# Rows of u and B for the scan's matmuls: 36 rows three partitions apart in two loads, or 40 rows in six loads

## The chip, the cores and the metric

One core of one Trainium2 chip runs the kernel. The metric is the device time of one execution in microseconds, lower is better; the kernel before takes 1117.4 us in the median of three runs (1115.65 to 1119.68).

## The reference

A Mamba block beside a small binary MLP, on x of shape 8 x 512 x 128, with E = 256 inner channels and N = 64 states. What matters here is the scan over T = 512 steps:

```python
normed = rmsnorm(layernorm(x)); x_z, z = split(normed @ in_proj_W)
xc = silu(conv(x_z)); dt = clip(softplus(xc @ dt_W + dt_b), 0.001, 0.1)
Bp, Cp = xc @ B_W, xc @ C_W
def step(h, ins):                        # h: 8 x 256 x 64, float32
    dA = exp(dt_t[..., None] * A)
    h = dA * h + dt_t[..., None] * B_t[:, None, :] * x_t[..., None]
    y_t = einsum('ben,bn->be', h, C_t)
```

Then y * silu(z), an output projection, a gated FFN, and the sum with the MLP and x.

## The kernel before

**Two stages.** A first stage handles the eight batches one after the other (`batches`): norms, projections, convolution, dt, and u = dt * xc. u and B are split into three bf16 parts each (`u_parts`, `b_parts`), whose nine products give the float32 product u * B on the matmul. The parts are stored to DRAM (`u_stage`, `b_stage`), dt as well (`dt_stage`). The second stage is the scan: 16 bodies of STEPS = 32 steps; three are written out, twelve stand in a loop of four turns with three bodies each, one is written out at the end.

**One step.** ScalarE (ACT) makes exp(dt * A) in place in `decay`, two steps at a time (L1011), two steps ahead, and copies half of the state out of PSUM (L1031). GpSimd (POOL) multiplies one half of the state with the decay (L593), VectorE (DVE) adds the product u * B that TensorE (PE) left in PSUM (L1238), and multiplies the other half in PSUM (L1227), onto which PE accumulates its product (L743 accumulates, L750 is the other half's). PE contracts the state with C (L798). Between these lie the output stages of the steps before (`finish_groups`).

**The rows of a product.** A product matmul contracts over 64 partitions, 0 to 63 for one half (`rows(0)`) and 64 to 127 for the other. 18 of the 64 hold a pair (part i of u, part j of B) for one of two batches; the rest is zero, set once. `moving` holds u, `b_rows` holds B with two layouts `hq` of the halves. The 36 rows of one `hq` stand three partitions apart from 10 + hq on (`product_rows`), both halves in one load. A chunk has TC = 16 steps and two buffers `cb`; for each chunk and `hq` there is one `load_u` (L194) and one `load_b` (L201), so 4 loads for 16 steps. In `moving` both `hq` have rows of their own.

**The queue.** All DMAs are issued by SyncE (SP), in program order. Besides the chunks it loads the decay: for each two steps one pair of loads of 512 KB (L392), into one of NDEC = 6 slots, as soon as `self_state` says that the slot's old steps are done. In one body (32 steps) SP issues 32 decay loads, 8 chunk loads, 2 `x_in` and 2 `out`. In `body` the loads of `hq` 0 stand ahead of the decay loads for steps 2 and 4, those of `hq` 1 behind these and ahead of the one for step 6; the same again 16 steps later. PE waits in `wait_chunk` for all loads of a chunk, ACT for its two decay loads.

**Between the stages.** SP stores for the last batch u (L417), issues the first four decay loads, stores B and the last part of u, waits until all have landed (L431), and issues the loads of chunk 0, eight decay loads, the loads of chunk 1.

## Time and profile before

| | us |
|---|---|
| median of three runs | 1117.4 |
| the profiled execution, its own time | 1104.51 |
| its span, first to last instruction | 1102.7 |
| PE, DVE, ACT, POOL busy | 965.8, 915.7, 922.8, 849.0 |
| mean granted TensorE clock | 0.952 |
| DMA moved | 327.40 MB, mean 297 GB/s |

The busy times are shares of one span: four engines are each busy for 77% to 88% of it, so none is alone the bound, and the stage that is looked at decides. The profiled execution is 12.9 us (1.2%) shorter than the median of the runs; sums below are made against it and then moved to the median.

### The profile page before, as it was taken

To read this page: it belongs to the slowest core of one execution; us is meant where nothing else is said; L and a number is where in the kernel's file an instruction comes from. 1 tells how busy PE (TensorE), PEld (TensorE's weight loads), DVE (VectorE), ACT (ScalarE), POOL (GpSimd) and SP (SyncE) were. 2 spreads that over 40 slices of the span, in tenths; PEclk is the share of its full clock that TensorE was granted. 3 is DMA by queue.
4 is the path that set the end of the run, shared out by engine and by line. 5 is a ranking of instruction groups with operands and counts; after the bars stand their busy time and mean duration, and the time that the engine had idled before them with its cause. 6 is when DMAs were issued, how large, how long until landed. Compare 5 with 4: busy or idle time off the path is not lost.

```text
span 1102.7 us, 27634 instructions
## 1 busy us (share of the span) xinstructions
PE 965.8 (88%) x8006; PEld 425.0 (39%) x8006; DVE 915.7 (83%) x2035; ACT 922.8 (84%) x1125; POOL 849.0 (77%) x1216
## 2 busy tenths in 40 slices
PE   5988983668999999997999997999999899999898
PEld 3565540113343433332334343334333334343436
DVE  5677663798989999997999997898998799899992
ACT  1656775689999999997999997999998899999981
POOL 6555523688888888897898887888888798889880
PEclk9999996679999999999999999899999899999999
DMA  5234358999999999998899999899999799999940
GB/s 140 81 139 165 142 202 300 327 319 353 341 345 344 338 355 350 344 352 316 315 355 354 345 348 344 290 346 358 339 350 344 272 354 352 345 343 350 350 158 11
DMA packets 76759, 327.40 MB, mean 297 GB/s; under 512 B 13472, under 2 KB 32800, under 8 KB 41504
## 3 DMA queue, kind: packets, MB, share of 16 engines
q1 hardware_dynamic: 76576, 325.30, 83.1%
q8 instruction: 73, 1.20, 0.4%
q14 instruction: 110, 0.90, 0.2%
HBM read 303.24 MB, written 22.02 MB: 295 GB/s over the span
## 4 chain that ended last, share of the span: by engine, by line
PE 32%; DVE 26%; POOL 19%; issue 14%; ACT 3%; DMA 3%; SPq 2%; DVEq 1%; POOLq 0%; ACTq 0%
POOL decayed L593 13%; PE ps L798 11%; DVE ps L1227 8%; PE ps L743 7%; DVE state L1238 6%; PE ps L883 5%; PE ps L897 5%; DVE h L1335 2%; DVE soft L1153 2%; DMA decay<-dt_stage 1%; POOL soft L543 1%; PE ps L861 1%; PE ps L869 1%; ACT state L1031 1%; DVE gated L1300 1%
## 5 line engine op out<-in xcount | busy, mean ns | idle before, releaser
L593 POOL TENSOR_TENSOR decayed<-decay,state 128x256 f32<-128x256 f32 x1024 | 726.6, 735 | 158.4 <-DVE state L1238 113.9
L1011 ACT ACTIVATE decay<-decay,a_col 128x2048 f32<-128x2048 f32 x256 | 513.9, 2008 | 31.8 <-DMA decay<-dt_stage 18.5
L1238 DVE TENSOR_TENSOR state<-decayed,ps 128x256 f32<-128x256 f32 x1024 | 405.7, 416 | 62.7 <-POOL decayed L593 41.1
L1227 DVE TENSOR_TENSOR ps<-decay,ps 128x512 f32<-128x512 f32 x512 | 352.3, 688 | 38.9 <-ACT state L1031 12.2
L798 PE MATMUL ps<-state,c_cols 128*32 128x256 f32 x4096 | 341.8, 407 | 0.0
L1031 ACT COPY state<-ps 128x512 f32<-128x512 f32 x512 | 288.3, 588 | 57.0 <-issue 37.6
L743 PE MATMUL ps<-moving,b_rows 64*128 64x256 bf16 x1024 | 206.4, 283 | 91.9 <-DVE ps L1227 88.9
L750 PE MATMUL ps<-moving,b_rows 64*128 64x256 bf16 x1024 | 207.4, 284 | 12.2 <-DMA b_rows<-b_stage 12.2
L883 PE MATMUL ps<-h,w 128*128 128x256 f32 x512 | 175.9, 429 | 0.8 <-DVE h L1335 0.8
L743 PEld LDWEIGHTS ps<-moving,b_rows 64*128 64x128 bf16 x1024 | 58.2, 95 | 268.9 <-DVE ps L1227 164.1
L798 PEld LDWEIGHTS ps<-state,c_cols 128*32 128x32 f32 x4096 | 82.4, 110 | 115.0 <-issue 104.5
L883 PEld LDWEIGHTS ps<-h,w 128*128 128x128 f32 x512 | 79.7, 191 | 92.8 <-issue 89.7
L750 PEld LDWEIGHTS ps<-moving,b_rows 64*128 64x128 bf16 x1024 | 57.5, 95 | 12.6 <-DMA moving<-u_stage 12.5
L652 PE MATMUL ps<-n_feat,w_tap 128*128 128x512 f32 x128 | 58.9, 614 | 1.0 <-ACT n_feat L917 1.0
L897 PE MATMUL ps<-w,h 128*128 128x128 f32 x256 | 44.6, 299 | 0.3 <-ACT h L1071 0.3
L848 PE MATMUL ps<-xn_feat,w 128*128 128x256 f32 x128 | 44.2, 429 | 0.3 <-DVE result L1344 0.2
L679 PE MATMUL ps<-w_dt,xc_feat 128*128 128x256 f32 x128 | 35.9, 439 | 8.5 <-ACT xc_feat L927 8.5
L897 PEld LDWEIGHTS ps<-w,h 128*128 128x128 f32 x256 | 33.5, 191 | 24.8 <-issue 24.0
L679 PEld LDWEIGHTS ps<-w_dt,xc_feat 128*128 128x128 f32 x128 | 32.1, 328 | 12.3 <-ACT xc_feat L927 10.3
L652 PEld LDWEIGHTS ps<-n_feat,w_tap 128*128 128x128 f32 x128 | 24.6, 198 | 29.8 <-issue 29.8
L1153 DVE TENSOR_TENSOR soft<-soft 128x1024 f32<-128x1024 f32 x8 | 20.8, 2602 | 16.3 <-POOL soft L543 16.3
L1113 DVE TENSOR_SCALAR normed<-x_tok,mean_var,nrm 128x128 f32<-128x128 f32 x32 | 19.9, 753 | 15.6 <-POOL nrm L534 15.6
(124 smaller groups left out, 813.3 us busy)
## 6 DMA issues: line engine op xcount, KB each, us to landing
decay<-dt_stage SPq DMA_DIRECT2D x512, 512.0 KB, 6.5
moving<-u_stage SPq DMA_DIRECT2D x64, 288.0 KB
b_stage<-b_parts SPq DMA_DIRECT2D x24, 384.0 KB, 3.7
b_rows<-b_stage SPq DMA_DIRECT2D x64, 144.0 KB
dt_stage<-dt_tok SPq DMA_DIRECT2D x8, 512.0 KB, 3.2
u_stage<-u_parts SPq DMA_DIRECT2D x8, 512.0 KB, 2.8
x_tok<-in_L_attn_x_dram SPq DMA_DIRECT2D x4, 512.0 KB, 3.6
u_stage<-u_parts SPq DMA_DIRECT2D x8, 256.0 KB, 2.1
```

The lines of the kernel that those rows point to most:

```text
L593: nc.gpsimd.tensor_tensor(decayed[:, p], decay[:, dec_slot(m, k), p, k % TS, :], state[:, (k - 1) % RING, p * E:(p + 1) * E], ALU.mult).th ...
L652: m = nc.tensor.matmul(ps[:, XC + h, :], w_tap[:, k, h * P:(h + 1) * P], n_feat[:, bass.ds(n, 1), k:k + T].rearrange("d o t -> d (o t)"), ...
L679: m = nc.tensor.matmul(ps[:, DTT + j // 2, (j % 2) * E:(j % 2 + 1) * E], xc_feat[:, bb, h, j:T:NJ], w_dt[:, h, :], start=(h == 0), stop=(h ...
L743: return nc.tensor.matmul(ps[:, acc_bank(m, k), p * E:(p + 1) * E], b_rows[rows(1), cb, p, kk, :], moving[rows(1), cb, kk, :], start=False ...
L750: return nc.tensor.matmul(ps[:, SELFP + k % 2, p * E:(p + 1) * E], b_rows[rows(0), cb, p, kk, :], moving[rows(0), cb, kk, :], start=True, ...
L798: m = nc.tensor.matmul(ps[q * 32:(q + 1) * 32, YP, 0:E], c_cols[:, cb, q, kk * 2 * TC:(kk + 1) * 2 * TC], state[:, k % RING, q * E:(q + 1) ...
L883: m = nc.tensor.matmul(ps[:, FB, c * GTOK:(c + 1) * GTOK], w1[:, n, f:f + P], h1[:, n, :], start=(n == 0), stop=(n == H1 // P - 1))
L897: m = nc.tensor.matmul(ps[:, FB, j * P:(j + 1) * P], terms[c][0][:, j * P:(j + 1) * P], terms[c][1], start=(c == 0), stop=(c == len(terms) ...
L1011: nc.scalar.activation(pair, pair, ACT.Exp, scale=a_col[:, 2:3]).then_inc(decay_ready, 1)
L1031: nc.scalar.copy(state[:, k % RING, SELF:QE], ps[:, acc_bank(m, k), :]).then_inc(acc_copied, 1)
L1227: nc.vector.tensor_tensor(ps[:, acc_bank(m, k), :].rearrange("p (q e) -> p q e", q=HQ), decay[:, dec_slot(m, k), HQ:Q, k % TS, :], ps[:, a ...
L1238: nc.vector.tensor_tensor(state[:, k % RING, p * E:(p + 1) * E], decayed[:, p], ps[:, SELFP + k % 2, p * E:(p + 1) * E], ALU.add).then_inc ...
```

## The change

For one `hq`, 32 rows stand on every second partition from 32 to 95, in 16 blocks of four partitions (two `hq`, two products). A block has one u row, loaded to both of its partitions, and two B rows. In DRAM the parts of u stand in the order 0, 2, 1, 2 (NS = 4 rows in place of 3); B has a plane for each of its parts, with the rows in the order of the blocks. This holds seven of nine products and one row of zeros (the blank, stored once from the zeroed `moving`). The two others (u parts 0 and 1 with B part 2) stand outside, on partitions 0 to 15 and 96 to 111, in four more loads of four rows each. So 40 rows in 6 loads for one `hq`, where there were 36 rows in 2. No matmul changes its shape.

```diff
-            sp.dma_start(moving[product_rows(hq), cb].rearrange("r t e -> r (t e)"),
-                         u_stage[hq, :, :, :, bass.ds(t, TC), :].rearrange("f b i t e -> (f b i) (t e)")
-                         .unsqueeze(1).broadcast_to([HALF * NP, NP, TC * E])
+            sp.dma_start(moving[window_rows(hq), cb].rearrange("r t e -> r (t e)"),
+                         u_stage[hq, :, :, :, bass.ds(t, TC), :].rearrange("f b s t e -> (f b s) (t e)")
+                         .unsqueeze(1).broadcast_to([BLOCKS, 2, TC * E])
                          ).then_inc(chunk_loaded[cb], 16)
...
-            sp.dma_start(b_rows[product_rows(hq), cb, hq].rearrange("r t n -> r (t n)"),
-                         b_stage[hq, :, :, :, :, bass.ds(t, TC), :].rearrange("f b i j t n -> (f b i j) (t n)")
+            sp.dma_start(b_rows[window_rows(hq), cb, hq].rearrange("r t n -> r (t n)"),
+                         b_stage[0:2, hq, :, :, :, bass.ds(t, TC), :].rearrange("r f b s t n -> (f b s) r (t n)")
                          ).then_inc(b_loaded[cb], 16)
+
+        def load_outer(sp, t, cb, hq):
+
+            for f in range(2):
+                sp.dma_start(moving[outer_rows(hq, f), cb].rearrange("r t e -> r (t e)"),
+                             u_stage[hq, f, :, 0:NP:2, bass.ds(t, TC), :].rearrange("b s t e -> (b s) (t e)")
+                             ).then_inc(chunk_loaded[cb], 16)
+                sp.dma_start(b_rows[outer_rows(hq, f), cb, hq].rearrange("r t n -> r (t n)"),
+                             b_stage[2, hq, f, :, 0:NP:2, bass.ds(t, TC), :].rearrange("b s t n -> (b s) (t n)")
+                             ).then_inc(b_loaded[cb], 16)
+
+        def load_chunk(sp, t, cb, hq):
+
+            load_u(sp, t, cb, hq)
+            load_b(sp, t, cb, hq)
+            load_outer(sp, t, cb, hq)
...
-                            [(u_parts, u_stage[q % HQ, q // HQ, bb], 0, 2, "u_mid_ready")]
-                            + [(b_parts, b_stage[q % HQ, q // HQ, bb, i], 0, NP, "b_split") for i in range(NP)]
-                            + [(u_parts, u_stage[q % HQ, q // HQ, bb], 2, 3, "u_split")]):
+                            (u_rows[0:NP:2], u_parts[:, bb, 0:2], 1, "u_mid_ready"),
+                            (b_planes[0, 0:NP], b_parts[:, bb, 0:1], NP, "b_split"),
+                            (b_planes[1, 0:NP], b_parts[:, bb, 1:2], NP, "b_split"),
+                            (b_planes[2, 0:NP:2], b_parts[:, bb, 2:3], 2, "b_split"),
+                            (b_planes[0, NP:NS], b_parts[:, bb, 2:3], 1, "b_split"),
+                            (u_rows[1:NS:2], u_parts[:, bb, 2:3], 2, "u_split"))):
...
+                            sp.wait_ge(blank_zeroed, 1)
+                            sp.dma_start(b_stage[1, :, :, :, NP].rearrange("a f b (p j) n -> p (a f b) (j n)", j=NJ),
+                                         moving[:, 1].rearrange("p t e -> p (t e)").rearrange("p (k n) -> p k n", k=B)
+                                         ).then_inc(blank_stored, 16)
```

On SP's queue, the last batch's stores and the loads of chunk 0, before (each row is an engine's instruction with its line, what it writes and reads, partitions x elements, and how many in a row):

```order
L417 DMA b_stage<-b_parts 128x3x512 x3
L417 DMA u_stage<-u_parts 128x1024
L194 DMA moving<-u_stage 36x1x4096
L201 DMA b_rows<-b_stage 36x2048
L194 DMA moving<-u_stage 36x1x4096
L201 DMA b_rows<-b_stage 36x2048
L392 DMA decay<-dt_stage 64x2048 x8
```

The same place on SP's queue after the change:

```order
L447 DMA b_stage<-b_parts 128x3x512 x2
L447 DMA b_stage<-b_parts 128x2x512
L447 DMA b_stage<-b_parts 128x512
L447 DMA u_stage<-u_parts 128x2x1024
L201 DMA moving<-u_stage 32x1x4096
L208 DMA b_rows<-b_stage 32x1x2048
L215 DMA moving<-u_stage 4x4096
L218 DMA b_rows<-b_stage 4x2048
L215 DMA moving<-u_stage 4x4096
L218 DMA b_rows<-b_stage 4x2048
```

Six such rows follow for the other `hq`, and then the eight decay loads: eight more issues stand ahead of these, and the last u store writes twice as much.

In a body of the scan, on SP's queue from the loads of `hq` 0 to the decay loads behind those of `hq` 1, before:

```order
L194 DMA moving<-u_stage 36x1x4096
L201 DMA b_rows<-b_stage 36x2048
L392 DMA decay<-dt_stage 64x2048 x4
L194 DMA moving<-u_stage 36x1x4096
L201 DMA b_rows<-b_stage 36x2048
L392 DMA decay<-dt_stage 64x2048 x12
```

And after, from the same place on:

```order
L201 DMA moving<-u_stage 32x1x4096
L208 DMA b_rows<-b_stage 32x1x2048
L215 DMA moving<-u_stage 4x4096
L218 DMA b_rows<-b_stage 4x2048
L215 DMA moving<-u_stage 4x4096
L218 DMA b_rows<-b_stage 4x2048
L415 DMA decay<-dt_stage 64x2048 x4
```

The next six chunk loads follow in the same way. Each group of decay loads now has four more issues ahead of it; the rows of the other engines differ in nothing but their line numbers.

## Rows read from the trace of the kernel before

**Rows 1.** The page: busy us (share of the span) by engine; the data queue.

```profile
PE 965.8 (88%) x8006; PEld 425.0 (39%) x8006; DVE 915.7 (83%) x2035; ACT 922.8 (84%) x1125; POOL 849.0 (77%) x1216
...
q1 hardware_dynamic: 76576, 325.30, 83.1%
```

**Rows 2.** Windows: stretch, its length, busy time by engine, clock, DMA share, GB/s.

```profile
160.00:173.50 13.50, 7.64 (x22) 3.07 (x20) 1.58 (x2) 10.97 (x14) 0.00 (x0) 0.93 0.88 301
173.50:184.00 10.50, 1.62 (x10) 0.61 (x10) 3.27 (x8) 0.53 (x1) 3.30 (x5) 0.50 0.73 231
184.00:195.00 11.00, 6.15 (x56) 1.62 (x56) 8.06 (x18) 9.33 (x11) 7.96 (x12) 0.64 1.02 342
195.00:206.00 11.00, 4.88 (x48) 1.15 (x44) 5.73 (x13) 6.19 (x7) 5.62 (x8) 0.67 1.00 367
...
357.00:520.00 163.00, 147.72 (x1394) 61.22 (x1390) 145.78 (x339) 151.12 (x185) 140.17 (x208) 1.00 0.98 349
```

**Rows 3.** ACT's waits by line, 166 to 206 us.

```profile
ACT decay L1011 <- DMA decay<-dt_stage: 16.5, 4, 10.7
```

**Rows 4.** ACT's waits by line, 206 to 1068 us, the scan's rest.

```profile
ACT decay L1011 <- DMA decay<-dt_stage: 2.0, 2, 1.4
```

**Rows 5.** SP's queue in time: start, us, what, how many; between the stages.

```profile
165.01 0.84 SPq L417 DMA_DIRECT2D u_stage<-u_parts  x1
173.53 0.95 SPq L194 DMA_DIRECT2D moving<-u_stage  x1
...
176.99 5.89 SPq L392 DMA_DIRECT2D decay<-dt_stage  x8
```

**Rows 6.** PE and ACT in time, the first that wait for these loads.

```profile
180.99 0.37 PE L750 MATMUL ps<-moving,b_rows 64*128 64x256 bf16 x1 [12.23 <-DMA b_rows<-b_stage]
...
184.70 2.00 ACT L1011 ACTIVATE decay<-decay,a_col 128x2048 f32<-128x2048 f32 x1 [10.67 <-DMA decay<-dt_stage]
```

**Rows 7.** SP's issues by line: duration ns min/median/max.

```profile
L392 SPq DMA_DIRECT2D decay<-dt_stage x512: 471/476/1482, 160.7 to 1055.8; - x171
...
L194 SPq DMA_DIRECT2D moving<-u_stage x64: 778/839/948, 173.5 to 1029.1; - x64
...
L201 SPq DMA_DIRECT2D b_rows<-b_stage x64: 730/778/797, 174.5 to 1029.9; - x64
...
L446 SPq DMA_DIRECT2D x_in<-in_L_attn_x_dram x32: 631/652/1099, 207.9 to 1044.0; - x32
```

**Rows 8.** DMA issues: count, KB each, median us to landing where known.

```profile
decay<-dt_stage SPq DMA_DIRECT2D x512, 512.0 KB, 6.5
moving<-u_stage SPq DMA_DIRECT2D x64, 288.0 KB
...
b_rows<-b_stage SPq DMA_DIRECT2D x64, 144.0 KB
```

**Rows 9.** SP's waits, 206 to 1068 us: total, times, longest.

```profile
SPq L392 <- DVE state L1238: 162.4, 98, 2.3
SPq L135 <- DVE state L1238: 134.0, 72, 5.6
```

**Rows 10.** SP's queue in time, one body of the scan.

```profile
701.15 1.63 SPq L452 DMA_DIRECT2D out_dram<-result  x2
...
717.98 0.84 SPq L194 DMA_DIRECT2D moving<-u_stage  x1
...
720.68 4.32 SPq L392 DMA_DIRECT2D decay<-dt_stage  x4
725.18 0.84 SPq L194 DMA_DIRECT2D moving<-u_stage  x1
726.22 0.77 SPq L201 DMA_DIRECT2D b_rows<-b_stage  x1
...
755.75 1.63 SPq L452 DMA_DIRECT2D out_dram<-result  x2
```

**Rows 11.** ACT in time, the exp of the pair issued at 666.6 us.

```profile
678.17 2.00 ACT L1011 ACTIVATE decay<-decay,a_col 128x2048 f32<-128x2048 f32 x1 [0.65 <-DMA decay<-dt_stage]
```

More of the change, by code:

```diff
@@ L46, in mamba_and_binary_mlp_block @@
     HROW = P // 2
[L47 to L50 removed]
+    NS = NP + 1
+    BLOCKS = 2 * HQ * NS
+    WFIRST, BSTEP = P // 4, P // 2 // BLOCKS
+    assert BLOCKS == 16 and BSTEP == 2 * HQ
     QE = Q * E
@@ L416, in store @@
                         wait_all(sp, [(S[ready], n + 1)])
-                        sp.dma_start(stage[i0:i1].rearrange("i (p j) e -> p i (j e)", j=NJ),
-                                     parts[:, bb, i0:i1].rearrange("p i j e -> p i (j e)")
+                        rows = parts.rearrange("p i j e -> p i (j e)")
+                        if copies > 1:
+                            rows = rows.broadcast_to([P, copies, rows.shape[-1]])
+                        sp.dma_start(stage.rearrange("i (p j) e -> p i (j e)", j=NJ), rows
                                      ).then_inc(S[f"parts_stored{bb}"], 16)
```

50 lines of the change are left out of this document (24 added, 26 removed).

## The prediction

> **What bounds the kernel now.** I read the page first. No engine is busy for more than 88% of the span, and the data queue fills 83.1% of what 16 DMA engines could do in it [rows 1]. A share over the whole span says little, so the windows come next: three stretches differ. Between the stages (160 to 184 us) all engines but ACT stand nearly idle while DMA moves 231 to 301 GB/s; from 184 to 206 us the scan has started and the DMA share is 1.0 at 342 and 367 GB/s; in the scan proper it is 0.98 at 349 GB/s, and PE, DVE, ACT are each busy over 89% [rows 2]. So the scan is tuned to engines and DMA at once. Who waits decides: ACT waits 16.5 us for decay loads before 206 us [rows 3] and only 2.0 us in the 862 us behind [rows 4]. Between the stages the path is: the last u store is issued at 165.01 us, SP sees it landed at 173.53, issues the four loads of chunk 0 until 176.99 [rows 5], PE starts at 180.99, and ACT, which has done two pairs, gets the third pair of decay at 184.70 [rows 6]. There DMA and SP set the time; in the scan they are hidden, but with little in hand.
>
> **The change part by part.**
>
> *Stores.* Each batch stores four planes of u in place of three, 256 KB more, in six issues in place of five; B's planes remain nine. For seven batches this lies beside engines' work, since SP only waits there for the next result. Behind the last batch it is on the path: 262 kB at the 301 GB/s of that stretch [rows 2] is +0.9 us. Bounds: 0.5 us (at 367 GB/s with some of it under the issue), 1.7 us (when the seventh batch's extra bytes are still queued too). The blank, 1 MB, is stored when SP has nothing else to do; were its DMA in the way, it would be 3 us of a stage in which DMA moves far less than it can. I cost it at nothing.
>
> *Chunk 0.* Twelve issues replace four. Four took 3.46 us (173.53 to 176.99), 0.81 us each and 0.05 between [rows 5]. How long SP needs for 32 or 4 rows, no row shows. The bounds are the shortest and the longest median: 0.476 us for the 64 rows of a decay load, 0.839 for 36 rows of u; `x_in` has 0.652 [rows 7]. For the 32-row loads, cut in 16 blocks, I take the decay's 0.48; for the four-row loads, an odd shape like `x_in`, 0.65. That gives 4 x 0.53 + 8 x 0.70 = 7.7 us, +4.3 us (ends: 12 x 0.53 = 6.3, +2.9; 12 x 0.89 = 10.7, +7.2). PE starts 4.0 us after SP is through with the old four [rows 5, 6]. A part of these 4.0 us is queueing: 864 KB within 3.5 us is more than the DMA engines move in it. Spread over 7.7 us that falls, by somewhat under 1 us. The eight decay loads are issued later by the same amount, and ACT waits for the first of them at once. I take +3.5 us of the 4.3 (ends 1.5 and 7).
>
> *Chunk 1.* 96 KB more in a full queue, at 342 GB/s [rows 2] +0.3 us. Its issues take 4.3 us longer too, but stand behind eight decay loads: 4.2 MB, 12 us of DMA at 342 GB/s, issued in 5.9 us [rows 5]. These 6 us in hand hide the 4.3. If the cover were gone, ACT's next waits would grow by what is left.
>
> *The scan, SP's time.* A body takes 54.6 us (701.15 to 755.75) and SP spends 1.03 us from one u load's issue to the next, of which 0.84 is the issue and 0.19 registers [rows 10, 7]. Eight 36-row issues become eight 32-row ones, 8 x (0.48 - 0.81) = -2.6 us, and 16 four-row ones come in, 16 x (0.65 + 0.19) = +13.4: +10.8 us a body. SP waits 296 us for DVE's state in 862 us [rows 9], 18.8 us a body (15.8 bodies). 8 us remain; at the upper price of 0.84 us it is 16.5 us with nothing saved, still under 18.8. So SP isn't the bound on average.
>
> *The scan, the late loads.* What is queued behind the six issues are the decay loads. With 4.7 us for six issues (2 x 0.67 + 4 x 0.84) where two took 2.1, the timeline of [rows 10] reads: `hq` 0 ends at 722.7 and not before 720.68, 2.0 us late; four decay loads back to back (4 x 0.66) bring SP to 725.4, 0.2 us late; `hq` 1 ends at 730.1 in place of 727.3, 2.8 us late. The pair behind it is the tightest of the body: the one issued at the same place at 666.6 us was waited for by ACT at 678.17 [rows 11]. But a load lands 6.5 us after its issue in the median [rows 8], and this one took 11.5: some 5 us of it is other loads ahead in full DMA engines. A load that is issued 2.8 us later then meets 2.8 us less of queue and lands at the same time. What stays is bytes: 432 KB for one `hq` [rows 8] become 480, 192 KB a body, 0.56 us at 349 GB/s. Over 15.8 bodies that is 8.9 us if DMA sets the pace, and 0 if the slack that left only 2.0 us of waits [rows 4] holds. As the tightest pairs have no slack already, I take two thirds, +6 us (ends: 0; 35, in the first rival).
>
> *PE.* Same matmuls on the same 64 partitions. PE waits for a chunk's last load in step 15 of 16; `hq` 1 is now issued by step 8 of them, with over 10 us to land. Nothing.
>
> The sum against the profile's own time: 0.9 + 3.5 + 0.3 + 6 = +10.7, 1104.5 to 1115.2 us. The median of the runs is 12.9 us above that execution; I add the same 10.7 to it: 1128.1 us.
>
> **A rule weighed against this.** In the rows, SP needs 0.84 and 0.78 us to issue 36 rows and 0.48 for 64 [rows 7]: the old loads are of an odd kind. The Trainium skill, "DMA: Bandwidth & Descriptors", section "Why a DMA increments its semaphore by 16 and not by 1", says that a load runs on the largest number of engines, up to 16, that divides the outer size on both sides. By that rule the old loads ran on 12 engines, the 32-row loads run on all 16, and four-row loads on the lowest four alone. No row of this profile tells engines apart. It speaks for the window and against the outer loads; by it the first rival holds, and the sum would be 1143 us rather than 1128.
>
> **The rivals.**
>
> *Four engines carry the outer loads (slower, more).* A load of four rows has four pieces to hand out; if each piece goes to one engine and always to the same ones, those hold back every decay load, which is landed only when its slowest engine is done. For: nothing in the change spreads them. Against: if the pieces are cut finer, it is nothing. Price: in a body such an engine moves 1024 KB of decay, 96 of the window, 384/4 = 96 of outer loads, 16 of `x_in` and `out`: 1232 KB, 1.262 MB. An engine moves 22.2 GB/s while busy (325.30 MB in 83.1% of 16 x 1102.7 us [rows 1]), or 22.9 at the peak of 367 [rows 2]: 56.8 or 55.1 us against 54.6. That is +0.5 to +2.2 us a body, +8 to +35; with its middle, 21, and the 4.7 us ahead of the scan, 1143 us. It decides once an engine's own load passes 54.6 us of work.
>
> *The better layout pays (faster).* Each block of four partitions is written by an engine of its own, and 16 rather than fewer engines share the window. If this lets all transfers run faster, the 16.5 and 2.0 us of ACT's waits [rows 3, 4] and part of PE's are there to win, and in the unprofiled runs perhaps some of the 12.9 us that the profile doesn't have. Against: the chunk loads are 1.7 MB of the 7.8 MB that move from 184 to 206 us; at half their cost that wins 2.4 us, less than the 4.7 that the issues and the stores cost. It decides only if decay loads gain too, by 8.1 of 18.5 us of waits for a gain beyond the bound. Price: 12 us won, 4.7 lost, 1110 us.
>
> The Trainium skill, "SBUF — State Buffer", section "Door 1: The DMA port swizzle", says that four neighbouring partitions share one DMA port and that 32 to 95 reach all 16 ports. By that rule the window is written without two engines on a port, but the decay loads' rows, nine times the bytes in a body, are where they were. It adds nothing to the sum.
>
> *Covered (no change).* Four-row issues at the lower price, queueing that shrinks as issues spread, slack that takes the bytes: 0.9 + 1.5 us, 1120 us.
>
> **How the numbers follow.** Forecast 43% (1122 to 1137), four engines 22% (1137 to 1158), faster 15% (1103 to 1114), covered 20%. 0.3% is 3.4 us, about what a measurement of this kernel tells from no change. Slower 0.65, same 0.20, faster 0.15. The range of 8 in 10 leaves out most of the faster case and the top of the four-engine one: 1113 to 1150.
>
> **What would show it.** In the changed profile: the last u store lands about 9.3 us after its issue, before 8.5; SP's issues of chunk 0 take some 7.7 us, with 0.48 and 0.65 us by line; PE's first product comes at about 185.5 us; ACT's waits for decay grow from 2.0 to some 8 us in the scan; SP's waits for the state fall by half. If these waits grow to tens of microseconds and a load's landing from 6.5 to over 8, four engines are overloaded. If the waits before 206 us fall under 16.5, the layout pays. Wrong would make me: four-row issues of over 1 us, which put SP itself over its 18.8 us, or a decay load that now lands sooner.

## The result, and the profile after

The changed kernel takes 1101.83 us (median of four runs, 1098.49 to 1103.92), the kernel before beside it 1116.53 us (1112.67 to 1119.68): ratio 0.9894, 95% interval 0.9845 to 0.9943. A second measurement later gave 1101.98 us and 0.9902 (0.9869 to 0.9934). It is faster by 1%; the forecast was 1128 us, slower, in a range from 1113 up. Both the direction and the range were wrong. A time below is the median of all executions of a kernel, but a ratio goes by those within 1.5% of its fastest; only for off_48 do the two differ by more than 1 us (1141.96 us over its six executions, 1133.62 over the three that count).

The page of the changed kernel, busy time and data queue, to set beside [rows 1]:

```profile
PE 954.4 (87%) x8006; PEld 422.2 (38%) x8006; DVE 914.5 (83%) x2035; ACT 922.1 (84%) x1125; POOL 847.5 (77%) x1216
...
q1 hardware_dynamic: 80816, 331.60, 81.2%
```

More bytes, 331.60 MB in place of 325.30, took a smaller share of a shorter span (1099.7 us). Not all of these bytes are in the scan: by the sizes of the loads a body of it has 18560 KB where it had 18368, 1.0% more; the rest is stores of the first stage. Bytes over (share x 16 x span) give what one DMA engine moves while it is busy: 23.2 GB/s where it was 22.2. I call this the engine's rate below; it is worked out in this way for each run.

The windows of the kernel after, the stretches of [rows 2]:

```profile
173.50:184.00 10.50, 0.00 (x0) 0.00 (x0) 1.07 (x2) 1.13 (x1) 1.40 (x2) 0.50 0.38 123
184.00:195.00 11.00, 5.41 (x38) 1.46 (x38) 7.02 (x16) 6.29 (x8) 6.68 (x10) 0.50 0.97 371
195.00:206.00 11.00, 6.34 (x72) 1.86 (x72) 8.27 (x19) 8.69 (x11) 8.83 (x13) 0.93 0.98 378
...
357.00:520.00 163.00, 147.38 (x1386) 61.00 (x1379) 145.32 (x338) 149.75 (x184) 139.72 (x206) 0.99 0.93 350
```

The first stretch became emptier (123 GB/s for 231): SP spends it on issues. The next two move 371 and 378 GB/s for 342 and 367. In the scan 350 GB/s need a share of 0.93 where 349 needed 0.98.

SP's queue between the stages after the change, against [rows 5]:

```profile
166.72 0.60 SPq L447 DMA_DIRECT2D u_stage<-u_parts  x1
175.06 0.60 SPq L201 DMA_DIRECT2D moving<-u_stage  x1
175.72 0.59 SPq L208 DMA_DIRECT2D b_rows<-b_stage  x1
176.35 0.71 SPq L215 DMA_DIRECT2D moving<-u_stage  x1
...
182.87 5.02 SPq L415 DMA_DIRECT2D decay<-dt_stage  x8
```

PE and ACT in time, against [rows 6]:

```profile
184.42 0.37 PE L779 MATMUL ps<-moving,b_rows 64*128 64x256 bf16 x1 [15.05 <-DMA b_rows<-b_stage]
188.28 2.00 ACT L1040 ACTIVATE decay<-decay,a_col 128x2048 f32<-128x2048 f32 x1 [13.64 <-DMA decay<-dt_stage]
...
203.13 2.00 ACT L1040 ACTIVATE decay<-decay,a_col 128x2048 f32<-128x2048 f32 x1 [2.31 <-DMA decay<-dt_stage]
```

And the exp of the kernel before that answers to the last of these:

```profile
202.77 2.00 ACT L1011 ACTIVATE decay<-decay,a_col 128x2048 f32<-128x2048 f32 x1 [3.77 <-DMA decay<-dt_stage]
```

Chunk 0 is issued from 175.06 to 182.87 us, 7.8 us where it was 3.5; PE starts 3.4 us later and ACT's third pair 3.6 us later; but 15 us on, at its seventh pair, ACT is at the same place in both profiles, 203.13 against 202.77. It looks as if what was lost between the stages came back at once. The control below doesn't bear this out: its seventh pair comes 4.4 us before that of the kernel after.

Then ACT's waits for decay from 206 to 1068 us in the kernel after [rows 4], and SP's waits in the same stretch [rows 9] (total, times, longest):

```profile
ACT decay L1040 <- DMA decay<-dt_stage: 4.6, 9, 0.9
```

```profile
SPq L137 <- DVE state L1267: 96.1, 58, 3.8
SPq L415 <- DVE state L1267: 33.7, 22, 2.3
```

ACT's 4.6 us are more than the 2.0 of [rows 4], so against that profile these waits show no gain; the control below says why. SP waits 130 us in place of 296: it has less time left, as forecast, but some. SP's issues by line, ns min/median/max, to set beside [rows 7]:

```profile
L415 SPq DMA_DIRECT2D decay<-dt_stage x512: 471/512/1837, 161.8 to 1052.9; - x171
...
L201 SPq DMA_DIRECT2D moving<-u_stage x64: 587/600/1052, 175.1 to 1026.2; - x64
...
L218 SPq DMA_DIRECT2D b_rows<-b_stage x128: 577/632/672, 177.1 to 1029.4; - x128
```

### The profile page after: what moved, and what is told of

It is laid out like the page before. It is cut to its first block, busy times and chain, and to the rows that moved or that the text cites. A ratio compares the mean times of both kernels' runs of the same rounds, so it can differ in the third digit from the quotient of the medians.

```text
span 1099.7 us, 28252 instructions
## 1 busy us (share of the span) xinstructions
PE 954.4 (87%) x8006; PEld 422.2 (38%) x8006; DVE 914.5 (83%) x2035; ACT 922.1 (84%) x1125; POOL 847.5 (77%) x1216
## 3 DMA queue, kind: packets, MB, share of 16 engines
q1 hardware_dynamic: 80816, 331.60, 81.2%
## 4 chain that ended last, share of the span: by engine, by line
PE 22%; DVE 21%; POOL 17%; issue 13%; ACT 2%; DVEq 1%; POOLq 0%; ACTq 0%
POOL decayed L622 15%; DVE ps L1256 8%; PE ps L827 7%; DVE state L1267 7%; PE ps L772 5%; PE ps L926 4%; PE ps L912 3%; DVE h L1364 2%; ACT state L1060 1%; PE ps L890 1%; PE ps L898 1%; DVE gated L1329 1%; POOL base L651 1%; POOL f_nrm L646 1%; POOL f_nrm L634 1%
## 5 line engine op out<-in xcount | busy, mean ns | idle before, releaser
L1256 DVE TENSOR_TENSOR ps<-decay,ps 128x512 f32<-128x512 f32 x512 | 352.5, 688 | 34.5 <-ACT state L1060 15.8
L827 PE MATMUL ps<-state,c_cols 128*32 128x256 f32 x4096 | 337.2, 402 | 0.0
L772 PE MATMUL ps<-moving,b_rows 64*128 64x256 bf16 x1024 | 204.2, 280 | 94.3 <-DVE ps L1256 91.3
L779 PE MATMUL ps<-moving,b_rows 64*128 64x256 bf16 x1024 | 205.2, 282 | 15.1 <-DMA b_rows<-b_stage 15.1
L912 PE MATMUL ps<-h,w 128*128 128x256 f32 x512 | 173.0, 423 | 0.8 <-DVE h L1364 0.8
L681 PE MATMUL ps<-n_feat,w_tap 128*128 128x512 f32 x128 | 57.8, 605 | 1.0 <-ACT n_feat L946 1.0
L708 PEld LDWEIGHTS ps<-w_dt,xc_feat 128*128 128x128 f32 x128 | 31.3, 328 | 15.1 <-ACT xc_feat L956 13.8
L1182 DVE TENSOR_TENSOR soft<-soft 128x1024 f32<-128x1024 f32 x8 | 20.8, 2601 | 16.3 <-POOL soft L572 16.3
L572 POOL TENSOR_TENSOR soft<-soft 128x1024 f32<-128x1024 f32 x7 | 17.2, 2453 | 20.6 <-DVE soft L1171 20.6
```

Of the source, the lines that this page charges most:

```text
L681: m = nc.tensor.matmul(ps[:, XC + h, :], w_tap[:, k, h * P:(h + 1) * P], n_feat[:, bass.ds(n, 1), k:k + T].rearrange("d o t -> d (o t)"), ...
L708: m = nc.tensor.matmul(ps[:, DTT + j // 2, (j % 2) * E:(j % 2 + 1) * E], xc_feat[:, bb, h, j:T:NJ], w_dt[:, h, :], start=(h == 0), stop=(h ...
L772: return nc.tensor.matmul(ps[:, acc_bank(m, k), p * E:(p + 1) * E], b_rows[rows(1), cb, p, kk, :], moving[rows(1), cb, kk, :], start=False ...
L779: return nc.tensor.matmul(ps[:, SELFP + k % 2, p * E:(p + 1) * E], b_rows[rows(0), cb, p, kk, :], moving[rows(0), cb, kk, :], start=True, ...
L827: m = nc.tensor.matmul(ps[q * 32:(q + 1) * 32, YP, 0:E], c_cols[:, cb, q, kk * 2 * TC:(kk + 1) * 2 * TC], state[:, k % RING, q * E:(q + 1) ...
L912: m = nc.tensor.matmul(ps[:, FB, c * GTOK:(c + 1) * GTOK], w1[:, n, f:f + P], h1[:, n, :], start=(n == 0), stop=(n == H1 // P - 1))
```

## The experiments

Each run stands beside runs of the kernel before on the same chip, and has a ratio to these. "On the blocks" means the window rows as in the kernel after (32 to 95), "off" means elsewhere. Where an edit leaves products out or changes them, the recorded expectation says so. The runs fell into four questions, in this order.

### 1. Was the profile of before a fair one, and does the place of the rows pay?

**before_again**, the kernel before once more.

> The kernel before, unchanged, as a control. Every theory expects a ratio of 1.00 within 0.5%, and this time a profile of an execution beside its others: if the profiled execution lies near 1104 us while the others lie near 1116, the 12.9 us that the first profile didn't have come from the execution and not from the kernel; if all lie near 1116, its trace shows in ACT's waits for decay loads in the scan (2.0 us before) what the first one did not.

It took 1110.48 us, ratio 0.9994 (0.9948 to 1.004). ACT's waits for decay in it, 206 to 1068 us:

```profile
ACT decay L1011 <- DMA decay<-dt_stage: 30.7, 27, 2.3
```

27 waits and 30.7 us, where the profile that the prediction read had two and 2.0 us [rows 4]. So the first profile was of an execution that happened to miss them. Its span is 1111.7 us, 9.0 more than the first. A decay load lands 7.7 us after its issue in the median, where the first profile had 6.5 [rows 8] and the kernel after has 6.4. The engine's rate is 21.7 GB/s here. The window that [rows 2] ends with reads:

```profile
357.00:520.00 163.00, 146.01 (x1340) 59.16 (x1339) 141.19 (x327) 144.94 (x178) 135.47 (x201) 0.97 0.99 338
```

A share of 0.99 moves 338 GB/s, where the first profile had 349 at 0.98 and the kernel after has 350 at 0.93.

The start of the scan is the other way round. ACT's seventh pair in the control:

```profile
198.77 2.00 ACT L1011 ACTIVATE decay<-decay,a_col 128x2048 f32<-128x2048 f32 x1 [3.40 <-DMA decay<-dt_stage]
```

That is 4.4 us before the kernel after, and so it stays: the tenth pair comes at 208.39 us in the control, at 212.39 in the first profile, at 212.66 in the kernel after. From there to the end of the span they need 903.3, 890.3 and 887.0 us. Against the control the change thus loses 4.3 us at the start and wins 16.3 us in the scan.

**off_port**, the window rows on every third partition:

```diff
-            first = WFIRST + hq
-            return slice(first, first + HQ * (2 * BLOCKS - 1) + 1, HQ)
+            first = 16 + hq
+            return slice(first, first + 3 * (2 * BLOCKS - 1) + 1, 3)
...
-            first = f * (P - WFIRST) + hq
+            first = f * 112 + hq
```

> The changed kernel with its 32 rows of one hq three partitions apart from 16 + hq on, so a block no longer stands on four partitions of its own; the same bytes, loads, order and issues, 16 blocks as before. Theory A (port): the gain comes from where the rows stand in SBUF; then this is back at the kernel before or slower, ratio 0.998 to 1.01, and a busy DMA engine moves about 22.2 GB/s again in place of 23.2. Theory B (spread): the gain comes from 16 even shares of a load, whatever partitions they go to; then the ratio remains about 0.989 and the rate 23.2.

1140.84 us, ratio 1.0225 (1.017 to 1.0279): 39 us more than the kernel after with the same bytes and the same issues. Its data queue, and ACT's waits in the scan:

```profile
q1 hardware_dynamic: 80816, 331.60, 83.1%
```

```profile
ACT decay L1040 <- DMA decay<-dt_stage: 52.0, 39, 3.6
```

The rate is 21.8 GB/s, for 23.2 on the blocks. The costs that the prediction feared are real here; on the blocks they don't show to this extent.

**no_outer**, the four-row loads left out on the blocks (`load_outer` isn't called, `LOADS = HQ`).

> The changed kernel without its four-row loads: the products of u parts 0 and 1 with B part 2 are left out, the rows stay zero. 32 issues of 50 KB and less are gone from two bodies' 48 chunk loads. If the four-row loads cost what I forecast (SP's time, four engines, first start), this is 3 us faster than the changed kernel at the first product and some 5 us at the end, ratio about 0.984; if they are hidden in the scan and the start is recovered, the ratio stays within 0.3% of the changed kernel's, 0.986 to 0.992.

1091.72 us, 0.98 (0.975 to 0.9849): the outer loads cost 10 us on the blocks.

**one_decay**, one decay load of 128 partitions in place of two of 64:

```diff
-                    for bb in range(2):
-                        sp.dma_start(decay[bb:P:2, slot].rearrange("n q t e -> n (q t e)"),
+                    sp.dma_start(decay[:, slot].rearrange("n q t e -> n (q t e)"),
```

> The changed kernel with one decay load of 128 rows (1 MB) for two steps in place of two of 64 rows (512 KB each). SP issues 16 fewer in a body. Theory A (port): an engine's share is eight neighbouring partitions in place of four of every second one, the same two ports' worth, so DMA's rate hardly changes and the gain is SP's time alone: ACT's waits for decay in the scan fall from 4.6 us towards 2, ratio 0.985 to 0.990. Theory C (SP's late issues are what is left of the cost): ratio under 0.985. If a larger load lands later (twice the bytes before ACT may start), it is slower: ratio over 0.992.

1101.3 us, 0.9884 (0.9838 to 0.9931). ACT's waits in the scan fell to 0.2 us and the time stayed: neither SP's decay issues nor what is left of ACT's waits sets the scan's pace after the change. (The recorded theory A takes a share to be eight neighbouring partitions; no row shows which partitions a share has.)

### 2. What do the outer loads cost, and where?

**off_no_outer**, off the blocks and without outer loads (both edits above).

> The kernel after with the window rows moved off their blocks (every third partition from 16 on, as in the run with the rows off port) and without the four-row loads, so two of the nine products are missing; four loads for a chunk, as in the kernel before. It gives the fourth corner of rows on or off their blocks, with or without outer loads. So far: on with 1101.8, on without 1091.7, off with 1140.8 us. If the place of the rows and the outer loads are two separate costs: 1140.8 - 10.1 = 1130 us (1125 to 1136). If the gain of the blocks is there only to hide what the outer loads cost (SP late, queues behind), the place costs little without them: under 1105 us. If the outer loads cost more where the queues are fuller: 1112 to 1122, about the kernel before.

1096.73 us, 0.9854 (0.9806 to 0.9902). This broke the picture that I had: the place is worth 39 us with the outer loads but 5 us without them, and the outer loads cost 44 us off the blocks but 10 on them. The two are no separate costs. Its queue, beside the kernel before:

```profile
q1 hardware_dynamic: 78768, 325.31, 84.5%
```

It moves the bytes of the kernel before in all (325.31 MB for 325.30), with no row on a block of its own, and is 1.5% faster. In a body it moves 1.0% less, 18176 KB for 18368, since some of its bytes are stores of the first stage; by the prediction's price for bytes that is at most 8.9 us of some 16. How the bytes are dealt out could be the rest: by the prediction's count the fullest engine has 1184 KB a body before, 1136 here, 1232 in the kernel after and with the rows off.

That count rests on the number of shares into which a load is cut, and the traces show that: they keep the increments by which DMA raises a load's semaphore while its parts land. On the semaphores of the chunk loads, a load of 36 rows has 13, one of 32 rows 16, one of four rows five, and one of 32 rows from eight source rows (eight_off below) nine. Wherever there are fewer than 16, one of them comes about 1.2 us after the issue, ahead of all data (in eight_off the loads issued at 183.11 and 183.88 us have theirs at 184.26 and 185.00, and no data of them has landed before 194.8). That leaves 12, 16, four and eight shares.

**outer_small**, one step of 16 in each outer load (`[outer_rows(hq, f), cb, 0:1]`, `bass.ds(t, 1)`).

> The kernel after, with the same eight four-row loads a chunk but one of 16 steps in each, so a sixteenth of their bytes and of their pieces' length (two of nine products are right in one step of 16 only). All issues stay. Leaving the loads out won 10.1 us. If SP's time for eight more issues is the cost: 1101 us, within 2. If their bytes, or the four shares in which they are carried, are the cost: 1092 to 1095 us, with ACT's waits for decay in the scan gone.

1100.76 us, 0.9884 (0.9836 to 0.9931).

**outer_wide**, each outer load 16 rows of a quarter of the length:

```diff
-                sp.dma_start(moving[outer_rows(hq, f), cb].rearrange("r t e -> r (t e)"),
-                             u_stage[hq, f, :, 0:NP:2, bass.ds(t, TC), :].rearrange("b s t e -> (b s) (t e)")
+                rows, part = slice(f * (P - WFIRST), f * (P - WFIRST) + BLOCKS), slice(hq * 4, hq * 4 + 4)
+                sp.dma_start(moving[rows, cb, part].rearrange("r t e -> r (t e)"),
+                             u_stage[hq, :, :, :, bass.ds(t, 4), :].rearrange("a b s t e -> (a b s) (t e)")
```

> The kernel after, with the same eight outer loads a chunk and the same bytes, each as 16 rows of a quarter of the length in place of four rows (their rows hold other parts than the products need, so the output differs). Issues and bytes stay, only the number of shares changes. If four shares that fall on few DMA engines are what the outer loads cost: 1092 to 1097 us, ACT's waits in the scan gone. If it is SP's issues or the bytes: 1100 to 1103 us.

1098.74 us, 0.9867 (0.982 to 0.9914). On the blocks the bytes and shares of the outer loads weigh 1 to 3 us, no more than the intervals. By elimination most of the 10 us stays with the mere issues; that isn't shown, and the profiled execution of outer_small took 1096.02 us, 4.7 less than its median.

**early**, four decay loads ahead of SP's wait for the stores:

```diff
+                for c in range(EARLY, EARLY + 2):
+                    load_dt(c, c, [])
                 sp.wait_ge(rows_zeroed, 2)
...
-                for c in range(EARLY, NDEC):
+                for c in range(EARLY + 2, NDEC):
```

> The kernel after, with four of the eight decay loads of the start issued ahead of SP's wait for the stores rather than behind chunk 0; nothing left out. In the profile of after ACT waits 13.6 us for the first of these eight, while DMA moves only 123 GB/s from 173.5 to 184 us. If order at the start is what ACT waits for: its wait near 188 us goes from 13.6 to about 8, PE's first product does not come later than 184.4 by more than 1 us, and 3 to 5 us are won, 1097 to 1099 us. If DMA as a whole sets the pace of the first pairs (1.0 share from 184 us on), the wait moves to the next pairs and the time stays at 1100 to 1103 us.

1098.82 us, 0.9864 (0.9817 to 0.9911), 3 us under the kernel after, as expected, though within the intervals. ACT's waits from 166 to 215 us fell from 16.4 to 4.2 us, and the window between the stages is filled:

```profile
173.50:184.00 10.50, 0.00 (x0) 0.00 (x0) 1.08 (x2) 2.71 (x2) 1.40 (x2) 0.50 0.77 301
```

It moves 301 GB/s for 123. ACT's tenth pair comes at 208.3 us, where it came at 212.7, and the span is 5.1 us shorter: what is won at the start is still there at the end.

### 3. Is it the fullest engine?

**eight_off**, the same 32 rows, each window load from eight source rows repeated four times:

```diff
-                         u_stage[hq, :, :, :, bass.ds(t, TC), :].rearrange("f b s t e -> (f b s) (t e)")
-                         .unsqueeze(1).broadcast_to([BLOCKS, 2, TC * E])
+                         u_stage[:, :, :, 0, bass.ds(t, TC), :].rearrange("q f b t e -> (q f b) (t e)")
+                         .unsqueeze(1).broadcast_to([8, 4, TC * E])
```

> The kernel with the window rows off their blocks and no four-row loads (1096.7 us), with one change: the source of each window load has eight outer rows, each repeated four times, in place of 16 repeated twice. Same rows written, same bytes, same four issues a chunk (the values differ and two products are missing). By the theory of the fullest engine such a load is cut in eight shares in place of 16, and a DMA engine's own bytes in a body set the time once rows stand off their blocks: 1136 KB for 1096.7, 1184 KB for 1114.5 (the kernel before, if its 36 rows are 12 shares), 1232 KB for 1140.8 (with the four-row loads in four shares). With eight shares it is 1024 + 192 + 16 = 1232 KB: 1135 to 1150 us, and tens of us of ACT's waits for decay in the scan. By the theory that all bytes count alike, or that the four-row loads were dear as issues: 1095 to 1099 us.

1145.29 us, 1.0304 (1.0257 to 1.0351), inside 1135 to 1150. Same bytes in a body, same four issues, no outer loads, and 49 us more than off_no_outer. The waits:

```profile
ACT decay L1040 <- DMA decay<-dt_stage: 60.5, 45, 3.2
```

off_no_outer had none in that stretch. SP's own time for such a load, off_no_outer first and then eight_off:

```profile
L201 SPq DMA_DIRECT2D moving<-u_stage x64: 591/620/1222, 174.5 to 1019.8; - x64
```

```profile
L201 SPq DMA_DIRECT2D moving<-u_stage x64: 664/737/1127, 174.8 to 1069.7; - x64
```

117 ns more for each of 128 loads are 15 us at most, not 49, and SP waits 344 us for DVE in this scan.

**eight_on**, the same edit on the blocks.

> The same change, eight outer rows repeated four times, in the kernel after without the four-row loads (1091.7 us), where the window rows stand on their blocks. The fullest engine has 1232 KB here too, but an engine's share now covers whole blocks of its own. If blocks of one engine each make every transfer faster, the extra bytes still fit: 1091 to 1100 us. If a block that is written by another engine than in the kernel after loses the whole gain: 1115 to 1140 us.

1144.29 us, 1.0304 (1.0248 to 1.036): a little beyond the second theory's 1115 to 1140. Rows on the blocks win nothing when eight shares write them, two blocks each by the order of the rows.

**off_48**, 48 rows on every second partition from 16 on, in 16 shares (`broadcast_to([BLOCKS, 3, ...])`).

> The kernel with the window rows off their blocks and no four-row loads (1096.7 us), with 48 rows on every second partition in place of 32 on every third: 16 blocks repeated three times, 16 shares, the same issues (the extra rows add products that don't belong; two products are missing). The fullest engine has 1024 + 144 + 16 = 1184 KB in a body, as in the kernel before, but all 16 have it, so all bytes are 3% more than before. If the fullest engine sets the time: 1110 to 1119 us. If the sum of the bytes sets it: over 1125 us. If shares of 12 were costly in themselves, not by their bytes: 1096 to 1105 us.

1133.62 us, 1.0201 (1.013 to 1.0271). Only the theory of the sum had a place for that (over 1125). The sum is 3.1% more in a body than before (18944 KB), all shares equal. Yet the trace shows unequal ones: of the 32 shares of a pair of decay loads the last lands 5.6 us after the first in the median, for 3.6 in off_no_outer. So some engines lag here although by the count none has more than another. Shares of three rows that lie across blocks may be the reason; that isn't shown, and the profiled execution was one of the longer (1148.90 us).

**off_wide**, off the blocks, outer loads in 16 shares.

> The kernel with the window rows off their blocks and four-row loads (1140.8 us), the outer loads as 16 rows of a quarter of the length (other values than the products need). Same bytes, same issues; the fullest engine has 1024 + 96 + 24 + 16 = 1160 KB in a body in place of 1232. If the fullest engine sets the time once rows are off their blocks: 1100 to 1112 us. If the outer loads cost 44 us there as issues or as bytes: 1135 to 1145 us.

1106.45 us, 0.9917 (0.9872 to 0.9962), inside 1100 to 1112. Of the 44 us that outer loads cost off the blocks, 34 go when the same bytes in as many issues are dealt out over 16 shares. With eight_off this says that the fullest engine was the bound off the blocks. The run also shows how little bytes alone do: it has all those of the kernel after, 1.0% more in a body than before, and no block of its own, and is faster than before; its 16 equal shares give the fullest engine 1160 KB for 1184. And beside outer_wide (0.9867) it shows the place alone, with equal shares: 5 to 8 us, within the intervals.

### 4. Is any block good, or only a share's own?

**shift_16**, window rows from 48 on (`first = WFIRST + 16 + hq`, outer rows at 112).

> The kernel after with its window rows moved up by 16 partitions, 48 to 111, and the outer rows behind at 112 (products fall into the wrong half, so the output differs). Each share still fills whole blocks of four partitions, one to one, but every block is written by another share than before. If one block for one share is enough: 1099 to 1104 us. If it has to be this one, the engine's own: 1120 to 1145 us. The run with eight shares on the blocks (1144.3 us) changed that and the engines' bytes together; this one changes it alone.

1167.78 us, 1.0501 (1.0448 to 1.0555): 66 us more than the kernel after, and beyond the range for the engine's own block. Its queue and ACT's waits in the scan:

```profile
q1 hardware_dynamic: 80816, 331.60, 83.0%
```

```profile
ACT decay L1040 <- DMA decay<-dt_stage: 79.7, 53, 4.9
```

The rate is 21.4 GB/s. Every share still has a block to itself, only another one (the outer rows of the second half moved too). So which block a share writes matters, more than whether it keeps to one.

**shift_2**, window rows two partitions lower (`WFIRST - 2 + hq`).

> The kernel after with its window rows moved down by two partitions, 30 to 93 in place of 32 to 95 (a few products fall into the wrong half, so the output differs). Rows stay on every second partition and shares, bytes and issues are the same, but every share now lies across two blocks of four partitions, and each block gets rows from two shares. If it is one block, one share that makes the kernel after fast: 1120 to 1145 us, as with every third partition (1140.8). If the spacing of the rows (every second in place of every third) was what counted: 1099 to 1104 us.

1108.57 us, 0.9951 (0.9926 to 0.9976), between the two expectations; the rate is 22.6 GB/s. By the order of the rows each share has one of its two still on its old block. It costs 7 us, not 39 or 66.

**decay_window**, decay loads by blocks, from the kernel without outer loads:

```diff
-                    for bb in range(2):
-                        sp.dma_start(decay[bb:P:2, slot].rearrange("n q t e -> n (q t e)"),
+                    for p0, p1 in ((P // 4, 3 * P // 4), (0, P // 4), (3 * P // 4, P)):
+                        sp.dma_start(decay[p0:p1, slot].rearrange("n q t e -> n (q t e)"),
```

> The kernel after without the four-row loads (1091.7 us), with each 1 MB of decay in three loads, partitions 32 to 95, 0 to 31 and 96 to 127, in place of two of every second partition. The middle one writes with each share the block that the window's rows have, so half of the decay's bytes lie there too. SP has half as many issues more, 253 in the scan at 0.5 us; it waits for DVE over 250 us there, which covers them. If the place of the decay rows counts as that of the window rows does, the data queue's share of the span falls under 82.5% by more than 3 points at the same bytes, ACT's waits near the start shrink, and the time is 1086 to 1090 us. If only the mixing with chunk loads counts: 1090 to 1096 us.

1481.13 us, 1.3291 (1.3216 to 1.3367): 389 us more, and no expectation came near. The data queue, a window of the scan, and SP's waits from 206 to 1068 us:

```profile
q1 hardware_dynamic: 82864, 325.32, 91.0%
```

```profile
357.00:520.00 163.00, 122.02 (x984) 47.22 (x976) 105.19 (x240) 107.04 (x129) 99.04 (x146) 0.87 1.02 240
```

```profile
SPq L414 <- DVE state L1266: 197.9, 94, 5.3
SPq L137 <- DVE state L1266: 158.9, 58, 5.5
```

The queue is full, at 240 GB/s, and SP has time left, so it isn't the issues: the engines move 15.1 GB/s each while busy, for 22.5 with the decay in two loads. Half of the decay's bytes now come in loads of 32 rows; if they are cut in 16 shares in order, two rows to a share, two shares write each block of four. I had looked at the middle load and forgotten the outer two. The last column is the median time from issue to landing, of the middle load and of the outer ones issued behind it:

```profile
decay<-dt_stage SPq DMA_DIRECT2D x256, 512.0 KB, 9.7
...
decay<-dt_stage SPq DMA_DIRECT2D x512, 256.0 KB, 14.7
```

The outer loads have half the bytes and take longer, but since they also queue behind the middle one, this alone doesn't show that they are the slow ones.

**early_one**, the two edits that leave nothing out together, early and one_decay.

> The kernel after with both edits that left the result whole: four of the eight decay loads of the start ahead of the wait for the stores (alone 1098.8 us), and one decay load of 1 MB for two steps in place of two of 512 KB (alone 1101.3 us). Nothing left out. If they add: 1098 us. If SP's time at the start is what the four-row loads cost (their leaving out won 10 us, cutting their bytes nearly nothing), the two together win more: 1094 to 1097 us.

1095.59 us, 0.9858 (0.9815 to 0.99). **after_again** and **early_one_again** were then run on one chip.

> The kernel after once more, beside its best variant on the same chip, to set one against the other: 1099 to 1104 us, ratio to the kernel before 0.984 to 0.992. If its gain over before were one chip's, the ratio comes near 1.

> The variant with four decay loads issued early and 1 MB decay loads once more: 1093 to 1098 us, 4 to 8 us under the kernel after beside it. If its 6 us were chance, within 2 us of it.

1101.98 us, 0.9902 (0.9869 to 0.9934), and 1096.97 us, 0.9856 (0.9824 to 0.9888): on one chip the variant is 5.0 us, 0.5%, under the kernel after. It is the fastest kernel here that leaves nothing out.

### All runs in one measure

For each run, the fullest engine's bytes in a body (decay 1024 KB, `x_in` and `out` 16, the window and outer loads by their shares) divided by the engine's rate give the time that this engine needs for a body, an estimate, since the rate is a mean over 16 engines. Two columns beside it are read from the packets and semaphores of the trace: the mean time of a DMA packet of 4096 bytes from 357 to 520 us (one row of B; no other load has that size), and the spread, which is the time from the first to the last landing among the 32 shares of a pair of decay loads, median from 206 to 1068 us (48 shares for decay_window). The last column is the time of the same profiled execution, not the median.

| run | fullest, KB | rate, GB/s | us a body | B row, ns | spread, us | its time, us |
|---|---|---|---|---|---|---|
| outer_small | 1142 | 22.9 | 51.0 | 164 | 3.0 | 1096.0 |
| no_outer | 1136 | 22.5 | 51.6 | 168 | 3.1 | 1094.9 |
| outer_wide | 1160 | 22.7 | 52.4 | 169 | 3.2 | 1097.7 |
| off_no_outer | 1136 | 22.0 | 52.9 | 261 | 3.6 | 1095.2 |
| after | 1232 | 23.2 | 54.4 | 162 | 3.2 | 1101.6 |
| off_wide | 1160 | 21.8 | 54.5 | 273 | 3.7 | 1110.0 |
| before | 1184 | 22.2 | 54.6 | 245 | 3.9 | 1104.5 |
| shift_2 | 1232 | 22.6 | 55.8 | 195 | 3.8 | 1111.3 |
| before_again | 1184 | 21.7 | 55.9 | 256 | 6.0 | 1113.6 |
| off_48 | 1184 | 21.1 | 57.4 | 273 | 5.6 | 1148.9 |
| off_port | 1232 | 21.8 | 57.8 | 239 | 5.2 | 1143.6 |
| eight_on | 1232 | 21.5 | 58.7 | 225 | 7.1 | 1141.9 |
| eight_off | 1232 | 21.4 | 59.0 | 250 | 7.5 | 1145.7 |
| shift_16 | 1232 | 21.4 | 59.1 | 271 | 5.4 | 1170.8 |
| decay_window | 1136 | 15.1 | 77.1 | 293 | 13.3 | 1482.1 |

The five runs that leave the chunk loads as in the kernel after have 22.9 to 23.2 GB/s.

Up to some 54.5 us the other engines of the scan seem to hide it (a body takes 54.6 us [rows 10]). Beyond, the excess times 15.8 bodies gives the growth only roughly: the time grows by half to all of it (off_port 51 us by the estimate and 42 measured, eight_off 71 and 44, shift_16 72 and 69). The estimate isn't independent of the time either: the queue's share is 81 to 84% in most runs, so that a longer span alone makes the rate smaller. The two columns from the trace don't have this fault, and they part the two causes. A row of B takes 162 to 169 ns where its share fills the block that it has in the kernel after, 195 where one of two rows does, and 225 to 293 everywhere else: this is the place. The spread is 3 to 4 us where all shares are equal. Four overfull shares leave it there while the rows stand on these blocks (after), and raise it to 5.2 us off them and to 5.4 in shift_16; eight raise it to 7 us and more on or off. This is the fullest engine. off_48 is the exception named above, and the kernel before has 3.9 us in one execution and 6.0 in the other. The kernel before lay at the edge or a little beyond it, the kernel after lies on it.

## Why the prediction was wrong

**The start: right.** The issues of chunk 0 took 7.8 us (7.7 forecast), PE's first product came at 184.42 us (185.5), the last u store landed 8.3 us after its issue (9.3 forecast, 8.5 before: the term of 0.9 us for the stores was nothing). By line a 32-row issue took 0.60 us, not 0.48, a four-row one 0.62, not 0.65; the errors cancel. ACT's third pair came 3.6 us late, as in the sum (+3.5). Beside the first profile ACT is level again at 203 us, since that execution lost another 5.8 us in waits there; beside the control it is 4.3 us late at its tenth pair, near the 4.7 us of the sum. That early keeps its gain to the end says the same.

**The scan: the step that failed.** "What stays is bytes: [...] 0.56 us at 349 GB/s [...] I take two thirds, +6 us". It takes the rate of the DMA engines as given and lets the change act on bytes alone. In the runs the bytes hardly count: off_wide has 1.0% more of them in a body and is 0.8% faster than before. What counts is how they are divided and where they go. Cut in 16 shares in place of 12, the old loads' bytes give the fullest engine less (off_no_outer and off_wide, 0.9854 and 0.9917). Then the four-row loads fill four engines again, which off the blocks costs 44 us (off_port, 1.0225) and on them 10 (0.9894), since there a row of B takes 162 ns in place of 239. So the share of the queue in the window from 357 to 520 us fell from 0.98 before to 0.93, with more bytes. In place of +6 us, the scan took 16.3 us less than the control's, and ACT's waits for decay went from 30.7 us to 4.6.

**The reading under it.** "Only 2.0 us in the 862 us behind", and slack "that left only 2.0 us of waits": that was one execution, and the shortest that I had. The text itself says that it lies 12.9 us under the median, and moves the sum by that without asking what these 12.9 us are made of. The control shows 30.7 us of DMA waits in another one. With them in view, there would have been more for "the better layout pays" to win than the 18.5 us that it was priced by.

**The rule on ports.** The prediction wrote of the block layout that "the decay loads' rows, nine times the bytes in a body, are where they were. It adds nothing to the sum." shift_16 shows that the same rows 16 partitions further, with the same bytes and issues, cost 66 us. Its rows of B take 271 ns for 162 (+67%), the packets of 8192 bytes, decay and u together, 370 for 345 (+7%); a decay load lands 7.4 us after its issue, for 6.4. The trace doesn't tell u from decay, but if a row of u, twice as long, slows as a row of B does, that is over half of the 7%. So the slow chunk rows hold up the decay loads that queue with them; whether decay rows are themselves written more slowly isn't shown. The second rival, better layout, was the right one, with its condition met ("only if decay loads gain too": they land after 6.4 us for the control's 7.7); its 1110 us were 8 too many. It was priced from the 22 us of the start alone, while the gain lies in the scan. "A decay load that now lands sooner" was also one of the two signs by which the prediction would know itself wrong.

**The first rival** was right in its mechanism and wrong for this layout: the fullest engine does set the time, but only where it is slow. On the blocks the rate rises to 23.2 GB/s, above the 22.9 that I took as the peak, and 1232 KB fit into a body. Off the blocks the run with four shares comes to 1140.8 us, and 1143 was the price; that is luck. At the 21.8 GB/s measured there the same sum gives 57.8 us a body, 50 us over the scan, and some 1172 us.

**SP's time in the scan: right.** SP's waits for the state fell from 296 to 130 us, by more than half, as forecast, and one_decay, with half as many decay issues, takes the same time.

**What stays open.** The increments count the shares, but that a share is always one engine's, and that a wrong block is slow because two engines meet at one entrance to the memory, no row shows; the runs show only which arrangement costs what. The Trainium skill, "DMA: Bandwidth & Descriptors", section "The descriptor swizzle", says that in a transfer over all 128 partitions each engine writes a port of its own, engine 0 the partitions 0 to 3 and 32 to 35, engine 8 those from 64 to 67 and 96 to 99. By that rule, and if share i is engine i's, the blocks from 32 to 95 in order are the engines 0 to 15 on their own ports, and 16 partitions further every one is on another's; after, shift_2 and shift_16 (1101.8, 1108.6, 1167.8 us) agree with it. But by the same rule the blocks from 48 to 111 put two shares each on the ports of engines 8 to 11 and none on those of 0 to 3. shift_16 changes both at once, so a port written twice by one load is a rival to a port that isn't the engine's own, and no run parts them. The Trainium skill, "SBUF — State Buffer", section "Door 1: The DMA port swizzle", adds that partitions 0 to 31 reach only 8 of 16 ports at all; the 240 GB/s of decay_window point the same way, but half of its bytes are in other loads, so no run here tests that rule alone. Also open are off_48, the part of the outer loads' 10 us that isn't at the start, and why one execution of the kernel before waits 2.0 us and another 30.7.

## What to carry to other kernels

Where small loads run beside large ones in a full DMA queue, their cost is not only their bytes but which block of partitions each share fills and what the fullest engine gets. Cut each load in 16 equal shares. Try the place of the rows as a variable of its own, since 16 partitions were worth 66 us here; in this kernel share i on the block of partitions from 32 + 4i was the best of those tried, and no run says which block it would be in another. Compare the time of one packet of the small loads, and the spread of a large load's landings, before and after: they tell the two causes apart. And when the profiled execution is 1% faster than the median, profile again before calling a stretch free of waits.

## What the runs showed of the hardware that I had not expected

Moving the window rows by 16 partitions, a twelfth of a body's bytes (1536 of 18560 KB, and 192 KB of outer rows with them), changed the time of the whole kernel by 6% (1101.8 to 1167.8 us); a 4096-byte row of B took 271 ns to write for 162, and the mean of a busy engine went from 23.2 to 21.4 GB/s. Splitting the decay loads so that half of their bytes come as 32 contiguous rows brought it to 15.1 GB/s, two thirds of the usual. A load of 36 rows is cut in 12 shares, one of 32 rows in 16, one of 32 rows from eight source rows in eight, and one of four rows in four. SP's issue of a load of 32 rows takes 620 ns in the median from 16 source rows and 737 ns from eight, both off the blocks.
